# In every step of the SP queue's program: the row fetch first, then the weight loads, the bias loads last

## The reference

```
for l in range(4):
    logits = x @ router_w[l] + router_b[l]; pick the best 2 of 4 experts, renormalise their weights
    xhat   = layernorm(x)
    for each chosen expert e:
        h = gelu((xhat * g[l,e] + b[l,e]) @ w1[l,e] + b1[l,e])      # 128 -> 512
        y = h @ w2[l,e] + b2[l,e]                                   # 512 -> 128
    x = sum over the chosen experts of weight * (x + y)
```

## Time and profile before

| | |
|---|---|
| median of 3 runs | 1839.06 us (1836.8 to 1841.24) |
| the profiled execution | 1830.5 us, its span 1828.8 us |
| busy share of the span | PE 85%, DVE 72%, ACT 67%, PEld 67%, POOL 47% |
| mean granted TensorE clock | 0.92 of full |
| moved by DMA | 323.99 MB, 177 GB/s on average |

### The profile page before, as it was taken

The page is one execution under the profiler, slowest core; times in us unless marked ns, Lnnn a source line. Parts: engine busy times, 40 slices in busy tenths (PEclk is TensorE's granted clock), DMA queues, the critical chain, the costliest instruction groups (busy, mean ns, idle before and its releaser), DMA issues.

```text
span 1828.8 us, 39992 instructions
## 1 busy us (share of the span) xinstructions
PE 1549.7 (85%) x11822; PEld 1230.0 (67%) x11822; DVE 1311.4 (72%) x4048; ACT 1233.3 (67%) x2137; POOL 858.5 (47%) x1431
## 2 busy tenths in 40 slices
PE   7999999633178998999889889988988999999992
PEld 4565665422167787778778777877877787777772
DVE  6999999533357777778768777877777777666662
ACT  4454454112087788778778777877877788898982
POOL 1111111255523454455444444544544457788776
PEclk9999999755589999999999999999999999999996
DMA  3899710122365676566566655656665655666751
GB/s 88 326 404 401 276 47 13 31 68 68 91 202 177 200 225 189 175 193 197 167 200 216 195 173 188 190 167 205 209 198 185 195 174 167 180 188 176 192 141 9
DMA packets 196047, 323.99 MB, mean 177 GB/s; under 512 B 47790, under 2 KB 128000, under 8 KB 195873
## 3 DMA queue, kind: packets, MB, share of 16 engines
q1 hardware_dynamic: 168608, 298.46, 49.3%
q0 software_dynamic: 27264, 23.54, 5.9%
HBM read 218.99 MB, written 108.71 MB: 179 GB/s over the span
## 4 chain that ended last, share of the span: by engine, by line
PE 44%; issue 8%; ACT 5%; SPq 5%; DMA 4%; DVE 4%; POOL 3%; POOLq 0%; ACTq 0%; DVEq 0%
PE ps_q L1361 7%; PE ps_h L1334 6%; PE ps_h L1336 6%; PE ps_h L1335 6%; PE ps_y L1349 6%; PE ps_y L1351 6%; PE ps_y L1350 6%; DMA wr<-in_L_ffn_w_dram 3%; ACT hh L990 2%; SPq L771 2%; ACT fin L1002 2%; PE ps_t L1322 1%; POOL out_dram L908 1%; DVE nrow L1101 1%; DVE row L1097 1%
## 5 line engine op out<-in xcount | busy, mean ns | idle before, releaser
L1065 DVE TENSOR_TENSOR hl<-hg,hh 128x1024 fp32r<-128x1024 f32 x336 | 409.0, 1221 | 281.7 <-ACT hh L990 281.5
L984 ACT ACTIVATE hg<-ps_h,bb 128x512 f32<-128x512 f32 x672 | 439.5, 683 | 157.0 <-PE ps_h L1336 151.4
L899 POOL DMA_INDIRECT regions<-nrow,posi x316 | 347.1, 1099 | 139.7 <-issue 74.5
L990 ACT ACTIVATE hh<-hg 128x1024 fp32r<-128x1024 f32 x336 | 354.9, 1056 | 2.8
L1334 PE MATMUL ps_h<-xTh,w1b 128*128 128x512 f32 x672 | 295.7, 440 | 2.1 <-DVE xTl L1081 1.4
L1361 PE MATMUL ps_q<-ir,yb 128*128 128x144 f32 x1344 | 215.8, 294 | 95.1 <-DVE nrow L1101 91.9
L1361 PEld LDWEIGHTS ps_q<-ir,yb 128*128 128x128 f32 x1344 | 191.6, 193 | 124.7 <-issue 109.0
L1336 PE MATMUL ps_h<-xTh,w1b 128*128 128x512 f32 x672 | 270.2, 402 | 0.0
L1335 PE MATMUL ps_h<-xTl,w1b 128*128 128x512 f32 x672 | 269.9, 402 | 0.0
L1349 PE MATMUL ps_y<-hh,w2b 128*128 128x512 f32 x672 | 268.9, 400 | 0.0
L1351 PE MATMUL ps_y<-hh,w2b 128*128 128x512 f32 x672 | 268.0, 399 | 0.0
(11 more groups left out here) (195 smaller groups left out, 2597.1 us busy)
## 6 DMA issues: line engine op xcount, KB each, us to landing
w1b<-w_split SPq DMA_DIRECT2D x168, 512.0 KB, 4.4
w2b<-w_split SPq DMA_DIRECT2D x168, 512.0 KB, 4.1
regions<-zero SPq DMA_DIRECT2D x98, 582.0 KB, 12.4
row<-regions SPq DMA_DIRECT2D x84, 294.0 KB, 4.4
w_split<-wst SPq DMA_DIRECT2D x32, 512.0 KB, 5.4
wr<-in_L_ffn_w_dram SPq DMA_DIRECT2D x32, 256.0 KB, 4.4
regions<-nrow,posi POOLq DMA_INDIRECT x316, 3.0
x<-in_L_attn_x_dram SPq DMA_DIRECT2D x16, 256.0 KB, 2.8
```

The lines of the kernel that those rows point to most:

```text
L899: g.indirect_dma_start(out=regions[layer % 2], out_offset=bass.IndirectOffsetOnAxis(ap=posi[r % 2][:, b:b + 1], axis=0), in_=nrow[r % 2][: ...
L984: a.activation(hg[c // 2 % PAIRS][:, c % 2 * TILE:(c % 2 + 1) * TILE], ps_h[c % BANKS][:], ACT.Gelu, bias=bb[n % 4][k // FC][:, k % FC:k % ...
L990: a.activation(hh[j % PAIRS][:], hg[j % PAIRS][:], ACT.Identity).then_inc(hi, 1)
L1065: v.tensor_tensor(hl[n][:], hg[n][:], hh[n][:].bitcast(F32), ALU.subtract).then_inc(lo, 1)
```

## The change

The order of the four groups of transfers in SP's steps: the row fetch, with its waits, now stands first, then `first_weights`, then `second_weights`, then the biases. Nothing else is changed: the same waits stand before the same transfers, and `raw_weights` and `store_weights` still stand behind all of them. The first loads, ahead of the loop, stay as they are.

```diff
                 for i in range(N):
+                    if i + 4 < N:
+                        rows_in(i + 4)
                     if i + 2 < N:
                         first_weights(i + 2)
-                        biases(i + 2)
                     if i + 1 < N:
                         second_weights(i + 1)
-                    if i + 4 < N:
-                        rows_in(i + 4)
+                    if i + 2 < N:
+                        biases(i + 2)
                     l, t = i // NTL, i % NTL
```

## The result

The changed kernel takes 1890.01 us (median of 4 runs, 1886.24 to 1892.5) against 1837.97 before (median of 4): a ratio of 1.0278, 95% interval 1.0256 to 1.0301. It is slower by 52 us, inside the range that was forecast and 12 us above the time forecast. The profiled execution's span is 1888.5 us.

What follows compares the result with a forecast made beforehand. SP was taken to wait nearly always for the end of the first products, its whole list delaying ACT in raw steps. Raw steps 25 plus layer ends 14 gave 39 us, so 1839.1 + 39 = 1878 us, range 1857 to 1906.

Steps and rivals of the forecast that it cites:

- Both costs: The forecast itself: raw steps lose 25 us and layer ends 14, together 39 us; chance 0.65.
- SP's wait moved from the first products to the update: Predicted sign in the profile after: SP waits mostly for DVE's update instead of the first products.
- Raw steps: Twelve steps that fetch raw weights: the second raw transfer lands 1.8 us later, costing 25 us, from 8 to 41.
- the count at 335 GB/s: Raw steps: 2,398 kB of rows and weights take 7.2 us, ending near 1333, as the second raw transfer is issued.
- the lone pair's 2.9 us: Raw steps: time the second raw transfer takes if the pair finds the queue empty; 3.4 us was assumed.
- the price of a later landing: Raw steps: 1.29 us later cost 1.51, a factor of 1.17, read from steps 27 and 52.
- The fit of the Trainium skill: Raw pair's transfer time: 2.0 us plus bytes at 436 GB/s, which would make the raw steps' part 14 us.
- Layer ends: Three steps with t = 18: w2 issued at 803.71 instead of 787.72, 4.8 us each, 14 in all, from 10 to 19.5.
- the clock was given 0.7 us: Layer ends: 0.7 us added to each step for PE's lower clock after its idle time.
- Only the layer ends cost: Rival: the raw pair lands under 1 us later; 22 us in all, 1861 us; chance 0.14.
- plain steps lose too: Rival: biases land late, gelu starts 0.5 us late in 69 steps, 34 us more, 1912 us; chance 0.14.
- Rows are what is late: Rival: rows fetched sooner end DVE's wait at layer ends, giving back 16 us, 1823 us; chance 0.03.

Runs made afterwards that it cites:

- e1: Changed kernel with the old order in the three steps with t = 17, whose row fetch is the next layer's first: 1866.33 us, ratio 1.0166 to the kernel before.
- e2: Changed kernel with the old order in the twelve raw steps (t = 2, 6, 10, 14): 1861.41 us, ratio 1.0135 to the kernel before.
- e3: Changed kernel with the old order in the twelve raw steps and the three with t = 17, new order in 69 others: 1837.55 us, ratio 1.0006.
- e4: Changed kernel with seven row buffers instead of six, order of transfers unchanged: 1835.84 us, ratio 0.9994 to the kernel before.
- e8: Kernel before with only the biases moved last (w1, w2, rows, biases): 1821.1 us, ratio 0.9922 to the kernel before.
- e7: Changed kernel with the biases back between w1 and w2, so only the row fetch is moved: 1913.17 us, ratio 1.0424 to the kernel before.

## Why the prediction was right, and where its sizes were off

*Direction and places.* Both costs were where the prediction put them, and nowhere else: e1 takes away one, e2 the other, e3 both and with them the whole loss. Both were forecast too small (39 us together, against 55 in the profiled executions and 52 in the medians), so no error made up for another. SP's wait moved from the first products to the update, as foreseen, and e4 shows that this wait is the cause in the raw steps.

*Raw steps, forecast 25 us, measured 32.5.* Two terms were small. The landing moved by 2.1 us in the mean of twelve (ACT's split starts 15.89 us into the step instead of 13.75), not 1.8: the second raw transfer went out 2.8 us later, as counted, but took 4.1 us and not the 3.4 taken; the queue had not drained as far as the count at 335 GB/s said. From the fetch to the second raw transfer in step 52 (us, busy of PE, PEld, DVE, ACT, POOL, granted clock, DMA share, GB/s):

```profile
1371.39:1379.38 7.99, 7.99 (x48) 6.84 (x47) 5.38 (x16) 3.46 (x6) 2.51 (x8) 1.00 0.81 274
```

At 274 GB/s these 7.99 us moved 2.19 MB of the 2.40 that the prediction took to be in; over the twelve raw steps it was 2.0 in the mean. The 0.4 MB left are 1.2 us at 335 GB/s, which with the lone pair's 2.9 us gives the 4.1 (an estimate from these numbers). The second term was the price of a later landing: 32.5 us over twelve landings moved by 2.14 is 1.27 us per us, not 1.17. This price is no constant: the forecast read it from two steps, and between the kernel before and e8 it is 0.8 (8.7 us for landings 0.89 sooner), between the changed kernel and e7 0.8 as well (21.6 us for 2.16), between the kernel before and e4 1.1 (20.4 us for 1.55 sooner). What else lies in the 1.27 stays open. The raw steps as a whole were inside the bounds of 8 to 41. The fit of the Trainium skill (DMA: Bandwidth & Descriptors, Anatomy of one DMA), made on another issuing path, gives about 2.6 us for this transfer as an estimate. That is shorter than any second raw transfer measured in the loop (least 3.2, in e8): these had other transfers around them.

*Layer ends, forecast 14 us, measured 22.2,* above the upper bound of 19.5. PE stops twice, first 7.9 to 8.4 us for w1, which the forecast did not name as a wait of its own, then 1.3 to 2.1 for w2; w2 comes last, so the sum over w2 holds, but its terms were too small. w2 was given its median of 4.1 us; issued behind w1 in one run it took 4.8, 5.8 and 5.3 at the three ends (until PE's second products start), and its median over the whole span is 5.2 in the changed kernel. And the clock was given 0.7 us. These stretches of step 18 (same columns) show more:

```profile
811.30:820.00 8.70, 0.78 (x5) 0.32 (x3) 3.60 (x16) 2.32 (x3) 2.02 (x4) 0.74 0.52 154
820.00:823.00 3.00, 1.74 (x4) 0.92 (x4) 2.47 (x8) 0.00 (x0) 1.09 (x4) 0.50 0.95 358
823.00:827.00 4.00, 4.00 (x12) 3.18 (x13) 0.00 (x0) 1.78 (x3) 0.00 (x0) 0.66 0.88 218
```

After 8 us with hardly any matmul, PE works at a granted clock of 0.50, the lower of its levels, through the first products, the second wait and the start of the second products. From 822.85 the step takes 13.9 us to its end, where 12.5 and the 0.7 were counted; at the other two ends it is 14.5 and 15.1. With the later w2 this makes 6.25 us at this end and 8 at the others, for 4.8 forecast.

*Gelu's wait for the biases* was not named in the prediction for the layer ends. At the end of layer 0 the tile's first products are done at 821.59, but gelu starts three us later, behind the biases issued at 820.29:

```profile
824.60 0.69 ACT L985 ACTIVATE hg<-ps_h,bb 128x512 f32<-128x512 f32 x1 [10.88 <-issue]
```

The wait is long (up to 12.8 us), but most of it lies in PE's own wait, and at none of the three ends does PE stand idle between the start of the second products and the end of the step. So no cost of it shows beside PE's waits, though no run takes it away by itself: in e7, with the biases ahead of w2, it falls to 8.1 to 8.8 us, but w2 goes out later there and the layer ends are longer, 83.2 us.

*The rivals.* "Only the layer ends cost" is out by e1 and e2, "plain steps lose too" by e3. "Rows are what is late" is out by the trace: the fetch at a layer's end went out 17.9 us into the step, as before, and DVE's wait for it is 4.93 us against 4.77. (In the prediction's reading of it 796.66 is the start of the last first product ahead of step 18, not its end, 797.06; the 19.15 us hold, as both ends of the step were taken so.)

## What to carry to other kernels

In a queue's program the order of transfers is first of all an order of waits: a transfer whose wait ends last, put first, holds back all the others, though here it is smaller than any one weight load behind it. Look for what stands at the end of the list and is wanted at once, here the raw weights: each us that they landed later cost 0.8 to 1.3, and fetching them a step sooner was worth 4%, more than any of the orders tried here. A load that is wanted a step later is hidden in plain steps, but rare steps with a long wait can cost much: here three of 84 made 22 of the 55 us.

## What the runs showed of the hardware

Two loads of 2.5 KB, moved from between w1 and w2 to between w2 and the raw pair, changed how long the pair's second half takes, from 6.2 us (e7) to 4.1 (changed kernel), though the pair goes out at the same time. With four 512 KB loads in one run w2's median landing is 5.2 us in the changed kernel and 5.3 in e8; with the two small loads in the middle it is 4.1 in the kernel before and 4.6 in e7. After PE had stood idle for 7.9 to 8.4 us at a layer's end, the granted clock was 0.50, and from the start of the second products the step took 13.9 to 15.1 us.
